# Attention scores and score maxima as products on quarters of TensorE's columns

## The chip, the cores and the metric

The kernel runs on one core of one Trainium2 chip. The metric is the device time of one execution in microseconds. Before the change it was 816.4, 816.55 and 818.32 us in three runs, median 816.55.

## The reference

The program is two decoder layers on 4 sequences of 256 tokens with 256 features, each layer an attention to a context of 1601 tokens, then a feed-forward part. The change lies in the attention of the second layer, which in the reference, with 16 heads of 16 features, is

```python
q = _qdq(x) @ _qdq(wq).T + bq
kv = cond @ wkv.T + bkv
k, v = jnp.split(kv, 2, axis=-1)
...
attn = jax.nn.softmax(jnp.einsum('bnhd,bmhd->bhnm', q, k) * scale, axis=-1)
o = jnp.einsum('bhnm,bmhd->bnhd', attn, v).reshape(B, N, C)
out = _qdq(o) @ _qdq(wp).T + bp
```

`_qdq` rounds to 8-bit integer steps, so the attention has to be exact to nearly float32. All of it has to be computed, over all 1601 keys; the second layer's feed-forward part follows.

## The kernel before

Queries and keys are each split into three bfloat16 parts, and six pairs of parts are stacked along the contraction (6 x 16 = 96 rows, `STACK_Q`, `STACK_K`), so that one bfloat16 product on 96 rows gives a float32-like score. `qst` holds the stacked queries of all sequences and heads, `kst` the stacked keys of two stages (a stage is half of the heads of one sequence).

The second layer's attention runs in a loop over 16 quads (four heads of one sequence) of 13 steps (`KT`, a tile of 128 keys, the last one of 65). In a step TensorE's stream holds, in this order:

- `scores` (L1066 to L1084): for each of four heads one product at L1080, stationary a tile of 128 keys (99 rows: three more carry minus the row maximum), moving the 256 queries of the head, output 128 x 256 into two PSUM banks that alternate by step. The first two heads, then the other two.
- `weigh` (L1086 to L1104) for the step before: the value products at L1101, float32. Each head has 17 stationary columns (16 values and a one for the denominator) and writes to its own group of 32 PSUM partitions, `bank(6)[32 * k:32 * k + VW]`; the four heads lie side by side on TensorE's columns. A float32 product is two instructions in the profile, so there are eight per step.
- `beside`: other work that a planner, `schedule` at L75, hands out by step: the keys (L878) and values (L888) of the next sequence, the transposes of the finished quad's output (`turn_out`, L1110), the tail of a finished sequence with its feed-forward part (`tail`, L1114 to L1187), and `shift` (L1056), which transposes the negated maxima on 3 columns at L1062. All but `shift` use 128 stationary columns.
- between these, `max_scores` (L978 to L991): the row maxima of the next quad need all scores once more, queries stationary, 128 x 400 or 401 keys to a product (L990), 32 of them to a quad. `pace` (L1222) places them evenly by the columns passed. They alternate between banks 0 and 1, and each waits until VectorE has reduced the last content of its bank.

The planner gives a step two to five maxima by the room it computes. The maxima for the first quad are made before the loop, in `first_maxima` (L993).

The other engines: VectorE reduces each block of maxima (L1669, `max_chunk`), forms the negated maxima after the last one of a quad (L1672 to L1680), and does the normalisation and the elementwise work of the tail. ScalarE makes the exponentials of a step in one instruction on 128 x 1024 (L1480, three buffers) and copies results from PSUM. GpSimd splits keys. SyncE issues all transfers. What a product waits for: scores of step i for the exponentials of step i - 2, value products for the exponentials of their step, a maximum for the reduction two before. Each group of products signals with its last instruction.

Of the kernel before, what the change touches and what calls it, by code (L numbers as in the profile page):

```python
# [27 lines left out]
P = 128  # L28
B, LQ, D = 4, 256, 256
# [20 lines left out]
HALF = H // 2  # L50
# [4 lines left out]
STACK_K = (0, 1, 0, 2, 0, 1)  # L55
SROWS = len(STACK_Q) * DH
VW = DH + 1
CH = [(0, 401), (401, 400), (801, 400), (1201, 400)]
MAGIC = float(1.5 * 2 ** 23)
LN_EPS = 1e-5  # L60
# [85 lines left out]
def program(nc, x_in, ctx_in, ctx0_in, seg_in, ident_in, tabs_in, kk_in, ones_in, wkvc_in, wkr_in, wkrs_in,  # L146
# [3 lines left out]
    with ExitStack() as ctx:  # L150
# [8 lines left out]
        def bank(i, n=1):  # L159
            return ps[:, i * 512:(i + n) * 512]  # L160
# [71 lines left out]
        kst = r1[:, 0:HALF * KEYS].bitcast(BF16).rearrange("p (r h k) -> p r h k", r=2, h=HALF)  # L232
        qst = r2[:, :].bitcast(BF16).rearrange("p (h t) -> p h t", h=H)
# [464 lines left out]
        def _(pe):  # L698
            mm = nc.tensor.matmul
# [7 lines left out]
            for c in range(FC):  # L707
                last = mm(bank(6), wkvc[:, c, :], ctx0[:, c, :], start=c == 0, stop=c == FC - 1)
            last.then_inc(kv_mm, 1)
            for b in range(B):  # L710
                for c in range(FC):
                    last = mm(bank(5)[:, b * KVC:(b + 1) * KVC], ctx0[:, c, b * K0:(b + 1) * K0], wkvc[:, c, 0:KVC],
                              start=c == 0, stop=c == FC - 1)
# [13 lines left out]
            for t in range(TILES):  # L727
# [3 lines left out]
                for c in range(FC):  # L731
                    last = nc.tensor.transpose(bank(2 + t % 2)[:, c * P:(c + 1) * P], xn[t % 2][:, c * P:(c + 1) * P],
                                               ident[:, :])
# [3 lines left out]
                if t >= 3 and t < 7:  # L737
                    for h in range(4 * (t - 3), 4 * (t - 3) + 4):
                        last = mm(bank(h // 8)[0:QC, (h % 8) * KVC:(h % 8 + 1) * KVC], wuq[:, h, :], wuk[:, h, :],
                                  start=True, stop=True)  # L740
# [6 lines left out]
            for hf in range(2):  # L747
                at = slice(hf * 512, (hf + 1) * 512)
                for h in range(H):
                    n = hf * H + h  # L750
# [7 lines left out]
                    if h % 2 == 1:  # L758
                        k = hf * (H // 2) + h // 2
                        if k >= 2:  # L760
                            pe.wait_ge(qb_ev, k - 1)
                        elif k == 1:
                            pe.wait_ge(kvt_ev, 1)
                        mm(bank(4 + k % 2), wqrs[:, h // 2, :], qcT[:, at], start=True,  # L764
                           stop=True).then_inc(qb_mm, 1)
# [209 lines left out]
                    last = nc.tensor.transpose(bank(7)[:, c * P:(c + 1) * P], qtok[:, c * P:(c + 1) * P], ident[:, :])  # L975
                last.then_inc(q1T_mm, 1)

            def max_scores(quad, n):  # L978

                b, s, u, c = quad // 4, quad // 2, n // len(CH), n % len(CH)  # L980
                h = 4 * (quad % 4) + u // 2
                ca = 8 * len(CH) * quad + n
                if n == 0:
                    pe.wait_ge(k_stk[quad % 4], 96 * (quad // 4 + 1))
                    pe.wait_ge(q_stk[b], 96)
                if ca >= 2:
                    pe.wait_ge(mx_rdy, ca - 1)
                a, m = CH[c]
                q0 = b * LQ + (u % 2) * P
                mm(bank(ca % 2)[:, 0:m], qst[0:SROWS, h, q0:q0 + P], kst[0:SROWS, s % 2, h % HALF, a:a + m],  # L990
                   start=True, stop=True).then_inc(mx_mm, 1)  # L991

            def first_maxima(t, third):  # L993

# [71 lines left out]
            def scores(quad, kt, first):  # L1066
                i, b, s = KT * quad + kt, quad // 4, quad // 2
                n = P if kt < KT - 1 else KLAST
                if first == 0:
                    if kt == 0:  # L1070
                        pe.wait_ge(sh_rdy, quad + 1)
                    if i == 0:
                        pe.wait_ge(ld_ones, 16)
                    if i == 1:
                        pe.wait_ge(v_ev, 2 * NV)
                    if i >= 2:
                        pe.wait_ge(ex_rdy, i - 1)
                for k in (first, first + 1):
                    h = 4 * (quad % 4) + k
                    last = mm(bank(2 + 2 * (i % 2), 2)[0:n, k * LQ:(k + 1) * LQ],  # L1080
                              kst[0:SROWS + 3, s % 2, h % HALF, kt * P:kt * P + n],
                              qst[0:SROWS + 3, h, b * LQ:(b + 1) * LQ], start=True, stop=True)
                if first == 2:
                    last.then_inc(sc_mm, 1)  # L1084

# [127 lines left out]
            for quad in range(QUADS + 2):  # L1213
                for kt in range(KT):
                    jobs = BESIDE.get((quad, kt), [])
                    maxima = [j for j in jobs if j[0] == "max"]
                    others = [j for j in jobs if j[0] != "max"]

                    total, count = step_work(others), len(maxima)
                    passed = [0]  # L1220

                    def pace(columns):  # L1222

                        passed[0] += columns
                        while maxima and (count - len(maxima)) * total < count * passed[0]:
                            max_scores(*maxima.pop(0)[1:])

                    if quad < QUADS:
                        pace(1)
                        scores(quad, kt, 0)  # L1230
                        pace(2 * LQ)
                        scores(quad, kt, 2)
                        pace(2 * LQ)
                        if quad or kt:
                            weigh(KT * quad + kt - 1)
                        pace(4 * LQ)
                    elif quad == QUADS and kt == 0:
                        weigh(STEPS - 1)
                    beside(others, pace)
                    while maxima:  # L1240
                        max_scores(*maxima.pop(0)[1:])


        @block.scalar
# [679 lines left out]
```

## Time and profile before

| | |
|---|---|
| median of 3 runs | 816.55 us (816.4 to 818.32) |
| the profiled execution | 814.17 us |
| its span | 812.4 us |
| TensorE busy | 753.3 us (93%), 5027 products |
| TensorE weight loads busy | 427.5 us (53%), 5027 |
| VectorE busy | 565.1 us (70%) |
| ScalarE busy | 383.6 us (47%) |
| GpSimd busy | 197.4 us (24%) |
| reductions of maxima (L1669) | 512 of 573 ns |
| exponentials (L1480) | 208 of 1024 ns |
| maxima (L990) | 512 of 341 ns |
| value products (L1101) | 1664 of 386 ns |
| scores (L1080) | 832 of 273 ns |

The profile is of one execution; times in it are counted from the start of its span. PE is TensorE, PEld its weight loads, DVE is VectorE, ACT ScalarE, POOL GpSimd, SP SyncE. The duration of a TensorE product runs from its start to the landing of its last column, and the next product starts before that; so the distance from start to start, not the duration, is what a product costs when the engine is full. "Busy" covers the durations, overlaps counted once. Idle time in brackets stands before the instruction, with what ended it.

### The profile page before, as it was taken

To read this page: it belongs to the slowest core of one execution; us is meant where nothing else is said; L and a number is where in the kernel's file an instruction comes from. 1 tells how busy PE (TensorE), PEld (TensorE's weight loads), DVE (VectorE), ACT (ScalarE), POOL (GpSimd) and SP (SyncE) were. 2 spreads that over 40 slices of the span, in tenths; PEclk is the share of its full clock that TensorE was granted. 3 is DMA by queue.
4 is the path that set the end of the run, shared out by engine and by line. 5 is a ranking of instruction groups with operands and counts; after the bars stand their busy time and mean duration, and the time that the engine had idled before them with its cause. 6 is when DMAs were issued, how large, how long until landed. Compare 5 with 4: busy or idle time off the path is not lost.

```text
span 812.4 us, 13087 instructions
## 1 busy us (share of the span) xinstructions
PE 753.3 (93%) x5027; PEld 427.5 (53%) x5027; DVE 565.1 (70%) x1290; ACT 383.6 (47%) x562; POOL 197.4 (24%) x208
## 2 busy tenths in 40 slices
PE   8999899978899989779999999999999999899996
PEld 4446677745556556554444455554455554345434
DVE  4887987712265675687787877777787777887814
ACT  2102435334333333216666666456665566574670
POOL 2497231312910321210310503100505002300000
PEclk9999999999999999989999999999999999999999
DMA  9300002004499142145065282650491810550000
GB/s 292 137 0 1 1 1 81 2 20 166 98 145 139 75 59 36 28 54 89 1 123 61 82 157 28 126 71 2 146 119 42 127 29 1 113 71 14 2 1 14
DMA packets 32476, 55.94 MB, mean 69 GB/s; under 512 B 11572, under 2 KB 20532, under 8 KB 31509
## 3 DMA queue, kind: packets, MB, share of 16 engines
q1 hardware_dynamic: 32408, 55.04, 34.2%
q8 instruction: 42, 0.69, 0.4%
q14 instruction: 26, 0.21, 0.1%
HBM read 42.56 MB, written 12.46 MB: 68 GB/s over the span
## 4 chain that ended last, share of the span: by engine, by line
PE 68%; DVE 18%; issue 6%; POOL 4%; ACT 2%; DMA 1%; SPq 0%; DVEq 0%; POOLq 0%; ACTq 0%
PE ps L1101 12%; PE ps L990 12%; PE ps L1080 9%; PE ps L878 6%; DVE small L1669 5%; PE ps L888 4%; PE ps L757 3%; PE ps L954 3%; PE ps L934 3%; PE ps L804 2%; PE ps L847 2%; PE ps L764 2%; PE ps L835 2%; DVE small L1619 1%; PE ps L1062 1%
## 5 line engine op out<-in xcount | busy, mean ns | idle before, releaser
L1669 DVE TENSOR_REDUCE small<-ps 128x1 f32<-128x400 f32 (+1 forms) x512 | 286.0, 573 | 82.6 <-PE ps L990 76.3
L1480 ACT ACTIVATE r<-ps 128x1024 f32<-128x1024 f32 (+1 forms) x208 | 212.6, 1024 | 89.1 <-PE ps L1080 86.1
L990 PE MATMUL ps<-r 96*128 96x400 bf16 (+1 forms) x512 | 170.8, 341 | 14.8 <-DVE small L1669 12.3
L1101 PE MATMUL ps<-r 128*17 128x256 f32 (+1 forms) x1664 | 130.7, 386 | 2.3 <-ACT r L1480 2.0
L1080 PE MATMUL ps<-r 99*128 99x256 bf16 (+1 forms) x832 | 126.0, 273 | 0.0
L990 PEld LDWEIGHTS ps<-r 96*128 96x128 bf16 x512 | 49.6, 97 | 126.9 <-DVE small L1669 93.3
L1080 PEld LDWEIGHTS ps<-r 99*128 99x128 bf16 (+1 forms) x832 | 81.5, 99 | 31.5 <-issue 9.3
L633 POOL TENSOR_TENSOR r<-r 128x400 bf16<-128x400 f32 (+1 forms) x32 | 29.4, 952 | 203.3 <-ACT r L1321 203.3
L934 PE MATMUL ps<-r,hT 128*128 128x512 f32 (+1 forms) x160 | 69.1, 564 | 0.0
L878 PE MATMUL ps<-r,wkvT 128*128 128x400 f32 (+1 forms) x128 | 53.3, 515 | 5.3 <-issue 5.3
L888 PE MATMUL ps<-wkvT,r 128*128 128x256 f32 (+1 forms) x208 | 57.1, 393 | 0.0
L1101 PEld LDWEIGHTS ps<-r 128*17 128x17 f32 (+1 forms) x1664 | 27.6, 95 | 51.8 <-issue 41.3
L622 POOL TENSOR_TENSOR r<-r,small 128x1024 f32<-128x1024 f32 x16 | 30.1, 1899 | 67.4 <-DVE small L1620 67.4
L614 POOL TENSOR_TENSOR r<-r 64x512 f32<-64x512 f32 x32 | 40.4, 1264 | 13.5 <-DVE r L1595 11.0
L1365 ACT ACTIVATE r<-ps,small 128x128 f32<-128x128 f32 x64 | 20.0, 364 | 50.1 <-DVE small L1646 27.6
L601 POOL TENSOR_TENSOR small<-small 128x1 f32<-128x1 f32 x24 | 14.0, 583 | 120.5 <-DVE small L1506 120.5
L888 PEld LDWEIGHTS ps<-wkvT,r 128*128 128x128 f32 (+1 forms) x208 | 39.1, 193 | 7.2 <-issue 0.3
L685 POOL TENSOR_TENSOR small<-small 128x2 f32<-128x2 f32 x4 | 2.8, 691 | 162.9 <-DVE small L1799 162.9
L1332 ACT ACTIVATE r<-ps 128x512 f32<-128x512 f32 (+1 forms) x28 | 15.9, 567 | 49.4 <-PE ps L888 49.3
L1303 ACT ACTIVATE r<-r 128x1024 f32<-128x1024 f32 x16 | 16.1, 1048 | 48.0 <-DVE r L1610 48.0
L1320 ACT ACTIVATE r<-ps,bk 128x400 f32<-128x400 f32 (+1 forms) x32 | 19.1, 597 | 41.3 <-PE ps L878 41.3
L934 PEld LDWEIGHTS ps<-r,hT 128*128 128x128 f32 x160 | 28.9, 196 | 18.3 <-issue 17.4
(201 smaller groups left out, 1023.9 us busy)
## 6 DMA issues: line engine op xcount, KB each, us to landing
r<-kscr SPq DMA_DIRECT2D x96, 200.1 KB, 8.8
kscr<-r SPq DMA_DIRECT2D x24, 400.2 KB, 4.0
r<-in_ctx_dram SPq DMA_DIRECT2D x4, 1601.0 KB, 6.9
r<-qscr SPq DMA_DIRECT2D x24, 128.0 KB, 5.2
r<-in_wo_dram SPq DMA_DIRECT2D x1, 2048.0 KB, 13.1
r<-in_gu_dram SPq DMA_DIRECT2D x1, 2048.0 KB, 7.7
qscr<-qpart SPq DMA_DIRECT2D x24, 64.0 KB, 1.7
x<-in_x_dram SPq DMA_DIRECT2D x1, 1024.0 KB, 5.4
```

The costliest lines, as they stand in the source:

```text
L614: nc.gpsimd.tensor_tensor(q, q, ropet[n % 2][at, :], ALU.add).then_inc(q_rdy, 1)
L622: nc.gpsimd.tensor_tensor(sm[t % 2][:, heads, :], sm[t % 2][:, heads, :], rec0[t % 2][:, heads].unsqueeze(2).to_broadcast([P, H // 2, K0]) ...
L633: last = nc.gpsimd.tensor_tensor(kpart[s][1][:, a:a + n], kf[s][:, a:a + n], kpart[s][0][:, a:a + n], ALU.subtract)
L757: mm(bank(n % 4), weff[:, h, :], qcT[:, at], start=True, stop=True).then_inc(qa_mm, 1)
L878: last = mm(bank(bnk)[:, 0:n], wkvT[:, k, (s % 2) * P:(s % 2 + 1) * P], ctxT[:, k, a:a + n], start=k == 0, stop=k == FC - 1)
L888: last = mm(bank(bnk)[0:n, (i % 2) * D:(i % 2 + 1) * D], ctxT[:, k, i * P:i * P + n], wkvT[:, k, D:2 * D], start=k == 0, stop=k == FC - 1)
L934: last = mm(bank(n % 3)[:, 0:w.shape[2]], hT[t % 2][:, k, :], w[:, k, :], start=k == 0, stop=k == FC - 1)
L990: mm(bank(ca % 2)[:, 0:m], qst[0:SROWS, h, q0:q0 + P], kst[0:SROWS, s % 2, h % HALF, a:a + m], start=True, stop=True).then_inc(mx_mm, 1)
L1080: last = mm(bank(2 + 2 * (i % 2), 2)[0:n, k * LQ:(k + 1) * LQ], kst[0:SROWS + 3, s % 2, h % HALF, kt * P:kt * P + n], qst[0:SROWS + 3, h, ...
L1101: last = mm(bank(6)[32 * k:32 * k + VW, 0:LQ], vx[0:n, b % 2, kt, h, :], pr[i % 3][0:n, k * LQ:(k + 1) * LQ], start=kt == 0, stop=kt == KT ...
L1480: fn(pr[i % 3][0:n, :], bank(2 + 2 * (i % 2), 2)[0:n, :], ACT.Exp, scale=SCALE1)\
L1669: v.tensor_reduce(mxc[quad % 2][:, n:n + 1], bank(ca % 2)[:, 0:m], AX_X, ALU.max).then_inc(mx_rdy, 1)
```

## The change

The scores and most of the maxima are issued as four products on 32 stationary columns each, that write to 32 PSUM partitions each, with the same moving operand; the value products have this form already. The last key tile (65 keys) is made of 32, 32 and 1. The maxima within the work of `beside` stay one product on 128 columns, as do those made before the loop; the others are parted. What is computed, the order of the work, the banks and the signals are the same: the last of the four products signals.

```diff
+QUARTER = P // 4
...
-            def max_scores(quad, n):
+            def max_scores(quad, n, parted=False):
...
-                mm(bank(ca % 2)[:, 0:m], qst[0:SROWS, h, q0:q0 + P], kst[0:SROWS, s % 2, h % HALF, a:a + m],
-                   start=True, stop=True).then_inc(mx_mm, 1)
+                width = QUARTER if parted else P
+                for r in range(0, P, width):
+                    last = mm(bank(ca % 2)[r:r + width, 0:m], qst[0:SROWS, h, q0 + r:q0 + r + width],
+                              kst[0:SROWS, s % 2, h % HALF, a:a + m], start=True, stop=True)
+                last.then_inc(mx_mm, 1)
...
                 for k in (first, first + 1):
                     h = 4 * (quad % 4) + k
-                    last = mm(bank(2 + 2 * (i % 2), 2)[0:n, k * LQ:(k + 1) * LQ],
-                              kst[0:SROWS + 3, s % 2, h % HALF, kt * P:kt * P + n],
-                              qst[0:SROWS + 3, h, b * LQ:(b + 1) * LQ], start=True, stop=True)
+                    for r in range(0, n, QUARTER):
+                        z = min(r + QUARTER, n)
+                        last = mm(bank(2 + 2 * (i % 2), 2)[r:z, k * LQ:(k + 1) * LQ],
+                                  kst[0:SROWS + 3, s % 2, h % HALF, kt * P + r:kt * P + z],
+                                  qst[0:SROWS + 3, h, b * LQ:(b + 1) * LQ], start=True, stop=True)
...
-                    def pace(columns):
+                    def pace(columns, parted=False):
 
                         passed[0] += columns
                         while maxima and (count - len(maxima)) * total < count * passed[0]:
-                            max_scores(*maxima.pop(0)[1:])
+                            max_scores(*maxima.pop(0)[1:], parted)
 
                     if quad < QUADS:
-                        pace(1)
+                        pace(1, parted=True)
                         scores(quad, kt, 0)
-                        pace(2 * LQ)
+                        pace(2 * LQ, parted=True)
                         scores(quad, kt, 2)
-                        pace(2 * LQ)
+                        pace(2 * LQ, parted=True)
                         if quad or kt:
                             weigh(KT * quad + kt - 1)
-                        pace(4 * LQ)
+                        pace(4 * LQ, parted=True)
                     elif quad == QUADS and kt == 0:
                         weigh(STEPS - 1)
                     beside(others, pace)
                     while maxima:
-                        max_scores(*maxima.pop(0)[1:])
+                        max_scores(*maxima.pop(0)[1:], True)
```

## Rows read from the trace of the kernel before

**Rows 1.** The page, busy time and instructions of each engine.

```profile
PE 753.3 (93%) x5027; PEld 427.5 (53%) x5027; DVE 565.1 (70%) x1290; ACT 383.6 (47%) x562; POOL 197.4 (24%) x208
```

**Rows 2.** Busy time by stretch, the whole loop: start:end, length, then busy by engine.

```profile
core 0: us, PE busy (x) PEld busy (x) DVE busy (x) ACT busy (x) POOL busy (x), PEclk, DMA share, GB/s
369.76:789.20 419.44, 406.55 (x3438) 203.17 (x3438) 319.41 (x701) 265.69 (x308) 68.00 (x75) 1.00 0.38 67
```

**Rows 3.** The chain of waits in order of time: start, length, what.

```profile
515.00 0.56 PE ps L1101 x8
515.55 0.28 PE ps L990
515.83 0.44 PE ps L1080 x4
516.27 0.17 PE ps L990
```

**Rows 4.** Timeline of TensorE, 513.8 to 515.5: start, length, engine, line, idle before.

```profile
513.84 0.38 PE L888 MATMUL ps<-wkvT,r 128*128 128x256 f32 x1
514.05 0.34 PE L990 MATMUL ps<-r 96*128 96x400 bf16 x1
514.23 0.60 PE L1080 MATMUL ps<-r 99*128 99x256 bf16 x4
514.66 0.34 PE L990 MATMUL ps<-r 96*128 96x400 bf16 x1
...
514.93 0.41 PE L1101 MATMUL ps<-r 128*17 128x256 f32 x4
...
514.93 0.63 PE L1101 MATMUL ps<-r 128*17 128x256 f32 x8
...
514.93 0.13 PEld L1101 LDWEIGHTS ps<-r 128*17 128x17 f32 x8 [0.27 <-issue]
515.48 0.10 PEld L990 LDWEIGHTS ps<-r 96*128 96x128 bf16 x1 [0.42 <-DVE small L1669]
```

**Rows 5.** Timeline of TensorE around a shift of the maxima, 695.0 to 696.0.

```profile
695.11 0.34 PE L990 MATMUL ps<-r 96*128 96x400 bf16 x1 [1.62 <-DVE small L1669]
695.39 0.61 PE L1062 MATMUL ps<-identb,nst 128*3 128x128 bf16 x8
695.93 0.34 PE L990 MATMUL ps<-r 96*128 96x400 bf16 x1
```

**Rows 6.** The page, costliest groups: count, busy, mean ns, idle before.

```profile
L1669 DVE TENSOR_REDUCE small<-ps 128x1 f32<-128x400 f32 (+1 forms) x512 | 286.0, 573 | 82.6 <-PE ps L990 76.3
...
L1101 PE MATMUL ps<-r 128*17 128x256 f32 (+1 forms) x1664 | 130.7, 386 | 2.3 <-ACT r L1480 2.0
```

**Rows 7.** Timeline of VectorE, 370.6 to 371.9.

```profile
370.70 1.19 DVE L1669 TENSOR_REDUCE small<-ps 128x1 f32<-128x400 f32 x2 [0.98 <-PE ps L990]
```

**Rows 8.** Busy time by stretch, each from value products to later ones, columns as rows 2.

```profile
369.76:371.20 1.44, 1.44 (x14) 0.64 (x14) 0.50 (x1) 0.92 (x2) 0.00 (x0) 1.00 1.25 112
766.10:767.55 1.45, 1.45 (x16) 0.64 (x15) 1.19 (x3) 0.81 (x2) 0.00 (x0) 1.00 0.00 0
371.20:373.05 1.85, 1.80 (x17) 0.73 (x16) 1.56 (x4) 1.25 (x2) 0.00 (x0) 1.00 1.27 108
384.62:385.89 1.27, 1.27 (x14) 0.54 (x13) 1.01 (x3) 0.73 (x1) 0.00 (x0) 1.00 0.04 13
738.74:740.01 1.27, 1.27 (x14) 0.54 (x13) 0.98 (x3) 0.96 (x1) 0.00 (x0) 1.00 0.00 0
781.24:783.52 2.28, 2.27 (x24) 0.88 (x24) 0.00 (x0) 2.05 (x2) 0.00 (x0) 1.00 0.00 0
```

**Rows 9.** Timeline of ScalarE in the last quad, 782.4 to 783.0.

```profile
782.45 1.02 ACT L1480 ACTIVATE r<-ps 128x1024 f32<-128x1024 f32 x1 [0.16 <-PE ps L1080]
```

**Rows 10.** Line L1062: duration in ns, minimum, median, maximum.

```profile
L1062 PE MATMUL ps<-identb,nst x128: 216/219/311, 364.8 to 771.7; 128*3 128x128 bf16 x128
```

**Rows 11.** The page, DMA queue that carries instructions: packets, MB, share.

```profile
q8 instruction: 42, 0.69, 0.4%
```

## Prediction

> **What bounds the kernel now.** I read the page first. TensorE is busy for 93% of the span, VectorE for 70%, ScalarE for 47% [rows 1]. The loop that the change is in runs from 369.76 to 789.20 us: 208 steps in 419.4 us, 2.02 us a step, on 16 quads of 13 steps, at a granted clock of 1.00 [rows 2]. "Busy" includes modelled ends, so next I took the chain of an undisturbed stretch apart, piece by piece, to see how long TensorE takes per piece and what it should take.
>
> A step with no other work and two maxima is, from 515.00 on, value products 0.56, maximum 0.28, four scores 0.44, maximum 0.17: 1.45 us, again and again, and TensorE stands in every piece [rows 3]. The two maxima are the same product and cost 0.17 or 0.28: the dear one follows the value products. The timeline shows why. A maximum (L990) at 514.05 is followed by scores 0.18 later, but the one at 514.66 by value products 0.27 later: 0.09 more. Of the eight value instructions (two passes for float32, four heads in four groups of 32 columns) four take 0.41 and eight 0.63, so the second pass starts about 0.21 after the first and is through with its columns another 0.21 later, at 0.42; the next weights are only loaded at 0.55 (515.48), and that load is no longer hidden: about 0.12 more. "Idle before" confirms it: 0.27 to 0.42 us without a weight load at either change [rows 4]. It is not float32 that costs: L888 at 513.84, float32 on all columns, is followed by a bfloat16 maximum 0.21 later, the time of its stream. Eight transposes on 3 columns start at 695.39 and a full-width product follows at 695.93; eight at the 0.055 worked out below are 0.44, so again 0.10 is lost [rows 5, 10]. So TensorE pays about 0.1 us each time it goes from products on all columns to products on a quarter, or back, and twice a step.
>
> **Part by part.** (1) Removed: changes of form. Following the order of emission in the code, I count 442 changes in the loop before and 149 after; those left stand around keys, values, turned outputs and the tail's products, which stay on all columns. 293 x 0.1 = 29 us of TensorE's time. That is not the gain, because other engines are close behind.
>
> (2) What comes next. VectorE's reduction takes 573 ns [rows 6]; two in a row take 1.19 us, so the pitch is 0.61, and an interval with three maxima lasts 1.85 us = 3 x 0.61 from one group of value products to the next: VectorE already sets it [rows 7, 8]. So by interval between value products:
> - Without full-width work, two maxima: 58 intervals of 1.44 or 1.45, the first from 369.76, the last from 766.10 [rows 8]. TensorE would need 0.42 + 0.44 + 2 x 0.17 = 1.20, VectorE needs 2 x 0.61 = 1.23. VectorE takes over: 0.21 saved each, 12.2 us.
> - The same with one maximum: 24 intervals of 1.27 to 1.38, the first from 384.62, the last from 738.74 [rows 8]. TensorE 1.03; ScalarE's exponentials, 1.02 each, come in pairs, and each pair waits for scores, which wait behind a maximum and the value products; I take 1.12. 0.15 saved, 3.6 us.
> - The last quad has no maxima: 2.28 for two steps, with ScalarE 0.16 idle between pairs [rows 8, 9]. The gap loses the 0.11 of one change; pitch 1.08 for 1.14, on 12 intervals: 0.7 us.
> - Three maxima (9 intervals), the steps with VectorE's long work (bias, scale) and the 15 with the shift of the maxima: nothing. At the shift, VectorE works off small operations after the last maximum, and TensorE's next maximum waits for it, 1.62 us in the case shown [rows 5]; the change reaches none of them.
> - The 74 intervals with full-width work: two changes before, two after. Nothing.
> Sum: 16.5 us.
>
> (3) Added: 2432 score products (832 become 3264; the last key tile has three parts, 32, 32 and 1) and 1263 for the 421 maxima that are parted; 59 maxima between full-width products and the 32 before the loop stay whole. Each brings a weight load, so 7390 instructions. What do they cost? Streams: the four groups of the value products start together (four in 0.41, where one alone has 386 ns in the mean [rows 4, 6]), so four quarters stream in the time of one if they don't share a limit; 0.11 for 256 columns, 0.17 for 400. Issue: eight weight loads of L1101 in 0.13 us, where the one of L990 has 0.10 alone [rows 4]: some 5 ns apart, and the products no more. From this end the cost is nil. The other end is the transposes on 3 columns: 0.61 for eight with 219 ns each is (0.61 - 0.22) / 7 = 0.055 a pair [rows 5, 10]; but 128 columns at 0.11 per 256 stream for 0.055 too, so that row is explained by its stream. I take the nearer row, the value products: quarters in the same four groups. Against it I set the stagger: the fourth group ends 0.02 after the first, which the 74 intervals that still change form pay, 1.5 us. That leaves 15. Waits: none is added, and only the fourth part signals, as one product did; nothing is moved past SP's or POOL's queues. Instructions fetched: 42 packets of 0.69 MB now for 10,054 loads and products [rows 1, 11], so some 30 packets more, at most one for each 5 us in quiet stretches; nothing in the trace is seen to wait for the present ones, and if that ends, each packet may cost a microsecond or so.
>
> **Forecast:** 15 us less. The profiled execution took 814.17 us for its span of 812.4, so 799.1; from the median of 816.55, 801.5. A measurement of this kernel can tell about 0.3% (2.4 us) from no change. Its own range: all 29 us is an end that VectorE's pitch excludes; 21 if waits at other places shrink too (795.5), 9 if quiet intervals meet other waits (807.5).
>
> **Rivals.** A, issue: a quarter's pair costs TensorE more than 27 ns, and four no longer fit in a score's 0.108. The place is the scores of every step, full-width ones too. With 0.055 a pair, the far end: scores 16 x 0.055 = 0.88 for 0.43, +94 us over 208 steps; maxima 0.22 for 0.17, +21; changes -29; less some 13 hidden where VectorE sets the interval: +73, so 890. It decides from about 32 ns a pair: (32 - 27) x 16 x 208 = 17 us, the whole gain. For it: no stretch shows more than eight narrow pairs together; a quiet step would need 32 pairs in 1.23 us, 38 ns each, and the queue may have been full in the bursts seen. Against it: those bursts are over five times faster. The Trainium skill, "TensorE: Matmul & The Clock Gate", under "Wait — 56ns, not 53.3ns?", says that with hardware decode off a matmul costs some 62 ns of microcode. By that rule, as an estimate, the scores alone would be 0.99 us a step, +116 us in all. The transposes at 0.055 a pair are below it, so the trace speaks against that mode. Chance 0.13.
>
> A2, streams: four bfloat16 quarters together get only the columns per time that four float32 ones get, 256 in 0.21. Scores +0.42 a step (+87), maxima +0.17 each (+70), changes -29: some 940. The bytes per time are those already seen, which speaks against it. 0.04.
>
> B, the cover is thinner: VectorE, at 1.19 of 1.44 us in quiet intervals, with its chains at shift and bias gives back half of the 12.2: 16.5 - 6.1 - 1.5 = 9 us or less saved, 807.5 to 813. 0.14.
>
> C, nothing: the drain belongs to the value products themselves (17 columns, float32), whatever stands beside them, so none goes. The transposes (3 columns, bfloat16) that lose the same 0.10 speak against it. 816 to 818. 0.07.
>
> **Chances.** Forecast 0.62, B 0.14, C 0.07, A 0.13, A2 0.04: faster by over 0.3% 0.76, within 0.07, slower 0.17. The range leaves out A and A2 and reaches to C: 795 to 817.
>
> **What would show it.** Value products followed by a maximum 0.42 to 0.45 after their start, with no 0.42 without a weight load; the three-line pattern of quiet intervals at 1.23 instead of 1.44, with VectorE's reductions 0.61 apart and the waits of L990 for VectorE longer in sum; last quad at 1.08; intervals with keys or values as long as before. A is right if the four parts of a score start more than 0.11 apart from the next head's and the product groups grow without an engine to wait for; C if 0.56 and 0.28 stand as they are. The forecast is wrong if the reductions stay further apart than 0.61 in quiet intervals though TensorE no longer changes form.

## The result and the profile after

The changed kernel is slower: 830.44 us (829.09 to 832.08, 4 runs) beside 816.47 (815.43 to 818.32, 4 runs) for the kernel before, a ratio of 1.0169 with a 95% interval of 1.0146 to 1.0191. The forecast was 801.5 in a range of 795 to 817. The profiled execution took 829.25 us, of which the span is 827.4 at a mean granted clock of 0.977; the kernel before had 814.17, 812.4 and 0.985. A few executions are longer at a lower granted clock whatever the kernel (824.91 us in one of 19 of the kernel before), and the ratios leave them out; of the version with quarters for the scores alone (below) that leaves one execution of four, 839.84 us.

In the lines that follow, the reductions of maxima are L1675 (L1669 before), the maxima L993 (L990), the scores L1086 (L1080), the value products L1107 (L1101), the exponentials L1486 (L1480), keys and values L879 and L889 (L878 and L888); in the kernels of the experiments some stand 2 to 10 lines further down. First the page of the kernel after: busy time, the instruction queue and the chain that ended last.

```profile
PE 740.6 (89%) x8721; PEld 458.0 (55%) x8722; DVE 569.0 (69%) x1290; ACT 381.8 (46%) x562; POOL 197.5 (24%) x208
...
q8 instruction: 71, 1.16, 0.6%
...
PE 56%; issue 18%; DVE 17%; POOL 4%; ACT 3%; DMA 1%; SPq 0%; POOLq 0%; DVEq 0%; ACTq 0%
```

Beside [rows 1] and [rows 11]: TensorE has 8721 products for 5027, and is busy for 12.7 us less although the span is 15 us longer. So it isn't TensorE's work that grew. VectorE's reductions (L1675) take the same 573 ns each. What did grow is the fetched code, 71 packets for 42, and "issue" on the chain, time in which an engine waits for nothing that the profile shows. The same line of the page of the kernel before had a third of it:

```profile
PE 68%; DVE 18%; issue 6%; POOL 4%; ACT 2%; DMA 1%; SPq 0%; DVEq 0%; POOLq 0%; ACTq 0%
```

**Where nothing interferes, the change does what was forecast.** The chain of waits of the kernel after through a quiet stretch (start, length, what), to be read against [rows 3]:

```profile
405.93 0.43 PE ps L1107 x8
406.37 0.17 PE ps L993 x4
406.54 0.44 PE ps L1086 x16
406.98 0.17 PE ps L993 x4
407.15 0.43 PE ps L1107 x8
```

Value products are followed by a maximum 0.43 us after their start, not 0.56, and no maximum costs 0.28 any more. One step is 407.15 - 405.93 = 1.22 us for 1.45. Busy time by stretch, with the columns of [rows 2], has the same step, an interval with three maxima, and the whole loop:

```profile
411.06:412.28 1.22, 1.22 (x36) 0.81 (x36) 1.15 (x3) 1.02 (x1) 0.00 (x0) 1.00 0.38 147
...
371.02:372.67 1.65, 1.58 (x43) 0.79 (x36) 1.58 (x4) 1.02 (x1) 0.00 (x0) 1.00 1.27 111
...
369.79:804.90 435.11, 395.19 (x7097) 234.24 (x7101) 323.29 (x701) 264.03 (x308) 68.11 (x75) 0.98 0.36 66
```

The loop takes 435 us for 419 [rows 2], and its granted clock is 0.98, not 1.00. The gain of the quiet steps is eaten somewhere else, and the clock points to stretches in which TensorE had fallen idle.

**Where the time went.** The same chain 20 us later:

```profile
426.21 0.21 PE ps L1086 x5
426.42 5.57 issue
431.99 0.83 PE ps L1086 x9
432.82 0.34 PE ps L993 x3
433.15 0.85 PE ps L1107 x6
```

In the middle of a head's scores TensorE stops for 5.57 us, no engine is waited for, and after it every piece takes twice its time: 0.85 for 0.43, 0.34 for 0.17. The stretches say why (the third column from the end is the granted clock):

```profile
426.42:431.99 5.57, 0.00 (x1) 0.00 (x1) 0.47 (x1) 0.00 (x0) 0.00 (x0) 0.83 1.06 123
432.00:436.90 4.90, 4.90 (x68) 3.65 (x72) 1.86 (x4) 2.05 (x2) 0.00 (x0) 0.50 0.96 115
```

During the gap the clock falls (0.83 in the mean), and for the 4.9 us after it it is 0.50, TensorE's level of 1.2 GHz instead of 2.4. There are five gaps of more than 1 us in the loop in which TensorE waits for no engine ("issue"), and none in the kernel before. In the timeline of TensorE they stand in brackets, as idle time before the first instruction behind them:

```profile
378.88 0.40 PE L1107 MATMUL ps<-r 128*17 128x256 f32 x3 [1.53 <-issue]
...
431.99 0.83 PE L1086 MATMUL ps<-r 99*32 99x256 bf16 x11 [5.57 <-issue]
...
496.73 0.52 PE L993 MATMUL ps<-r 96*32 96x400 bf16 x3 [4.02 <-issue]
...
619.28 0.34 PE L993 MATMUL ps<-r 96*32 96x401 bf16 x1 [1.49 <-issue]
...
739.10 0.52 PE L993 MATMUL ps<-r 96*32 96x401 bf16 x3 [5.98 <-issue]
```

Their sum is 18.6 us, and the three long ones are each followed by a stretch at a granted clock of 0.50, of 4.9, 5.0 and 5.0 us. What those stretches hold takes half of that at 1.00, so they cost another 7.5 us. Without both, the loop would take 435.1 - 18.6 - 7.5 = 409.0 us (an estimate), 10 less than before.

**What TensorE lacks is instructions.** The transfers of the kernel after from 415.3 to 428.2 (queue, kind: packets, MB, share of 16 engines):

```profile
q1 hardware_dynamic: 556, 1.45, 89.2%
...
r<-kscr SPq DMA_DIRECT2D x12, 200.1 KB, 10.6
```

There is no row for q8, the queue that carries instructions: no packet starts in 12.9 us. The first one starts in the next 0.2 us, at 428.24:

```profile
q8 instruction: 1, 0.02, 57.9%
```

It takes some 1.85 us (57.9% of 16 engines for 0.2 us), so it has landed at about 430.1, and TensorE goes on at 431.99. The other gaps end in the same way, 2.4 to 3.8 us after a packet starts.

A packet is 1.16 MB / 71 = 16 KB. The kernel has (20476 - 13087) = 7389 instructions more in 29 packets more, so 255 to a packet. A quiet step now issues 32 products and 32 loads in 1.22 us, so TensorE uses up a packet in 4.9 us. What moves meanwhile are the twelve reads of the stacked keys, 2.4 MB, which SyncE issues in one burst; its timeline:

```profile
416.35 5.48 SPq L549 DMA_DIRECT2D r<-kscr  x12
```

The kernel before has the same burst, and the trace had it too. Its transfers from 411.2 to 434.4:

```profile
q1 hardware_dynamic: 1265, 3.39, 91.2%
```

No packet starts for 23 us there either. But its quiet step issues 14 products and 14 loads in 1.45 us, so a packet lasts it 13 us.

A stretch without a packet isn't yet a late packet, since none may be due. How late one comes shows in the counts of products and loads before it, set against the same kernel without the key reads (below). There the packet of this place starts at 422.2 us, after 4994 products and loads. The kernel after had come as far at 420.8, but its packet starts at 428.24: 7.5 us late. It issued 226 more, until 426.4, and stopped. In the kernel before, the packet of the stretch starts without the reads after 3948 products and loads; with them it had come as far at 425.06, and the packet starts at 434.44, 9.4 us late. But 226 more instructions last it until about 438.7, so the packet is there in time. The delay is the same or longer; what differs is how long TensorE can go on.

### The profile page after: what moved, and what is told of

Its sections match the earlier page's. It is cut to its first block, busy times and chain, and to the rows that moved or that the text cites. A ratio compares the mean times of both kernels' runs of the same rounds, so it can differ in the third digit from the quotient of the medians.

```text
span 827.4 us, 20476 instructions
## 1 busy us (share of the span) xinstructions
PE 740.6 (89%) x8721; PEld 458.0 (55%) x8722; DVE 569.0 (69%) x1290; ACT 381.8 (46%) x562; POOL 197.5 (24%) x208
## 3 DMA queue, kind: packets, MB, share of 16 engines
q8 instruction: 71, 1.16, 0.6%
## 4 chain that ended last, share of the span: by engine, by line
PE 56%; issue 18%; DVE 17%; POOL 4%; ACT 3%; DMA 1%; SPq 0%; POOLq 0%; DVEq 0%; ACTq 0%
PE ps L993 9%; PE ps L1107 7%; PE ps L1086 6%; PE ps L879 6%; PE ps L889 4%; DVE small L1675 4%; PE ps L758 3%; PE ps L955 3%; PE ps L935 3%; PE ps L805 2%; PE ps L848 2%; PE ps L765 2%; ACT r L1486 2%; PE ps L836 1%; DVE small L1625 1%
## 5 line engine op out<-in xcount | busy, mean ns | idle before, releaser
L1675 DVE TENSOR_REDUCE small<-ps 128x1 f32<-128x400 f32 (+1 forms) x512 | 286.7, 573 | 94.1 <-PE ps L993 86.4
L1486 ACT ACTIVATE r<-ps 128x1024 f32<-128x1024 f32 (+1 forms) x208 | 210.9, 1023 | 103.8 <-PE ps L1086 101.1
L993 PE MATMUL ps<-r 96*32 96x400 bf16 (+3 forms) x1775 | 186.6, 343 | 28.5 <-DVE small L1675 14.7
L1107 PE MATMUL ps<-r 128*17 128x256 f32 (+1 forms) x1664 | 135.0, 388 | 7.0 <-ACT r L1486 4.6
L1086 PE MATMUL ps<-r 99*32 99x256 bf16 (+1 forms) x3264 | 132.5, 276 | 7.1 <-issue 6.0
L993 PEld LDWEIGHTS ps<-r 96*32 96x32 bf16 (+1 forms) x1775 | 57.5, 95 | 107.3 <-DVE small L1675 52.7
L1086 PEld LDWEIGHTS ps<-r 99*32 99x32 bf16 (+1 forms) x3264 | 91.2, 97 | 30.5 <-issue 6.9
L634 POOL TENSOR_TENSOR r<-r 128x400 bf16<-128x400 f32 (+1 forms) x32 | 29.4, 952 | 208.4 <-ACT r L1327 208.4
L879 PE MATMUL ps<-r,wkvT 128*128 128x400 f32 (+1 forms) x128 | 55.8, 535 | 5.4 <-issue 5.1
L1107 PEld LDWEIGHTS ps<-r 128*17 128x17 f32 (+1 forms) x1664 | 44.7, 98 | 27.4 <-ACT r L1486 16.0
L889 PE MATMUL ps<-wkvT,r 128*128 128x256 f32 (+1 forms) x208 | 58.4, 399 | 0.0
L889 PEld LDWEIGHTS ps<-wkvT,r 128*128 128x128 f32 (+1 forms) x208 | 38.0, 192 | 12.5 <-issue 4.8
L935 PEld LDWEIGHTS ps<-r,hT 128*128 128x128 f32 x160 | 28.9, 196 | 18.3 <-issue 17.3
L1326 ACT ACTIVATE r<-ps,bk 128x400 f32<-128x400 f32 (+1 forms) x32 | 19.1, 596 | 42.2 <-PE ps L879 42.2
```

The lines of the kernel that those rows point to most:

```text
L634: last = nc.gpsimd.tensor_tensor(kpart[s][1][:, a:a + n], kf[s][:, a:a + n], kpart[s][0][:, a:a + n], ALU.subtract)
L879: last = mm(bank(bnk)[:, 0:n], wkvT[:, k, (s % 2) * P:(s % 2 + 1) * P], ctxT[:, k, a:a + n], start=k == 0, stop=k == FC - 1)
L889: last = mm(bank(bnk)[0:n, (i % 2) * D:(i % 2 + 1) * D], ctxT[:, k, i * P:i * P + n], wkvT[:, k, D:2 * D], start=k == 0, stop=k == FC - 1)
L935: last = mm(bank(n % 3)[:, 0:w.shape[2]], hT[t % 2][:, k, :], w[:, k, :], start=k == 0, stop=k == FC - 1)
L993: last = mm(bank(ca % 2)[r:r + width, 0:m], qst[0:SROWS, h, q0 + r:q0 + r + width], kst[0:SROWS, s % 2, h % HALF, a:a + m], start=True, st ...
L1086: last = mm(bank(2 + 2 * (i % 2), 2)[r:z, k * LQ:(k + 1) * LQ], kst[0:SROWS + 3, s % 2, h % HALF, kt * P + r:kt * P + z], qst[0:SROWS + 3, ...
```

## Experiments

The expectations call theory F (fetch) S, for supply, and rival G I; in those for the three kernels with less added code, F stands for the price of a change of form instead.

**Theory F (fetch):** an instruction packet asked for during the burst of key reads comes late; TensorE, which now uses a packet in some 5 us of quiet steps, runs dry, and the pause takes the clock along. Rival G: the narrow pairs themselves cost more than their streams. Rival T: the burst slows the transfers or the memory as such, and the kernel before would gain from its absence as well. All medians stand beside those of the kernel before, run on the same chip.

**The reads one at a time, in both kernels.** SyncE waits for the landing of each read before it issues the next.

```diff
                                 .then_inc(k_stk[quad % 4], 16)
+                        if s >= 2:
+                            sp.wait_ge(k_stk[quad % 4], 96 * (quad // 4) + 16 * (g + 1))
```

After:

> The changed kernel, but each of the 12 reads of restacked keys (200 KB each) waits for the landing of the one before, so that the DMA queues never hold more than one. Theory S (instruction supply: TensorE runs dry because its instruction packets queue behind these bursts; the quarter form itself does what was forecast): the gaps of 2 to 6 us on TensorE that end shortly after a late instruction packet go, and with them the stretches at half clock behind them; 797 to 806 us. Rival I (the quarters themselves cost TensorE more, or the gaps have another cause): 827 to 833 us. Rival K (keys come too late when paced): slower than 833, with TensorE waiting for restacked keys.

Before:

> The same pacing in the kernel before, as control. Theory S: with 256 instructions to a packet and fewer than half as many used per us, nothing ran dry before, so 815 to 818 us. Rival: if the bursts slow the kernel before too (through SBUF or queues), some us less, and then e1's gain is partly this.

Measured: the kernel after 819.87 (815.78 to 821.15), the one before 825.05 (822.92 to 827.63), beside 816.38; ratios 1.0043 (1.0013 to 1.0074) and 1.0114 (1.0077 to 1.015). So one edit makes the one kernel 10.6 us faster and the other 8.7 us slower, and no gap above 1 us without an engine or a transfer to wait for is left in either. Both miss their expectations (797 to 806, and 815 to 818), because the keys now come late. The waits of TensorE (in total, times, longest), of the kernel after:

```profile
PE ps L995 <- DMA r<-kscr: 10.9, 3, 7.0
```

The kernel before has 9.6 us of the same wait. Some 10 us of new waits in each: the test was blunt, though its direction speaks for F and against T.

**No reads at all, in both kernels.** The stages from the third on take the keys that the first two left in place; the twelve reads of each of those stages aren't made, so the scores of the later sequences are of other keys.

```diff
-                        sp.wait_ge(k_stk[quad % 4], 96 * (s // 2))
+                        sp.wait_ge(k_stk[quad % 4], 96)
...
-                    for g, j in enumerate(STACK_K):
+                    for g, j in enumerate(STACK_K if s < 2 else ()):
...
-                    pe.wait_ge(k_stk[quad % 4], 96 * (quad // 4 + 1))
+                    pe.wait_ge(k_stk[quad % 4], 96)
```

After:

> The changed kernel without the reads that restack keys for stages 2 to 7 (the scores of later sequences are then made from the first stages' keys: that part of the computation is left out). Theory S: as paced or 1 to 3 us better, 796 to 803 us, no gap without an engine to wait for. Rival I: 825 to 832 us.

Before:

> The same reads left out of the kernel before, as control. Theory S: within 3 us of the kernel before, 813 to 817 us. If it gains much more, the bursts cost something besides instruction supply.

Measured: after 808.12 (807.11 to 808.56), ratio 0.9909 (0.9884 to 0.9934); before 816.71 (814.09 to 821.22), ratio 1.0016 (0.9995 to 1.0038), beside 816.38. The reads cost the kernel before nothing that can be measured and the kernel after 22 us. The kernel after is 5 us above the 796 to 803 that was expected without them, since other losses stay (below). This rules out T, and as the only explanation it rules out G, since the pairs are all still there. In this run the loop takes 411 us. One gap is left, 1.56 us at 380.

**Less added code.** Three kernels change the form of a part only. Quarters for the scores, whole maxima (4864 instructions more than before, 638 changes of form for 149):

```diff
-                width = QUARTER if parted else P
+                width = P
```

> Scores as quarters, all maxima whole. By the order of emission that is 638 changes of form in the loop, against 442 before and 149 with both parted; 4864 more instructions than before. Theory F (what a quarter saves is the change of form, about 0.1 us each, where nothing else sets the step): the scores alone lose, up to 20 us for the 196 changes more, and some instruction gaps beside: 828 to 845 us, quiet steps with two maxima at 1.55 to 1.7 us. Rival P (quarters are faster by themselves, whatever stands beside them): below 816.

Whole scores, quarters for the maxima (2526 more, 563 changes):

```diff
-                    for r in range(0, n, QUARTER):
-                        z = min(r + QUARTER, n)
+                    for r in range(0, n, P):
+                        z = min(r + P, n)
```

> Maxima as quarters, scores whole: 563 changes of form, 2526 more instructions than before. Theory F: quiet steps with two maxima keep two changes (maximum to scores, scores to maximum) and stay near 1.44, those with three get more; 815 to 828 us. Rival P: about half of the gain of both parts, 808 to 812.

Halves of 64 columns for both:

```diff
-QUARTER = P // 4
+QUARTER = P // 2
```

> Scores and maxima on halves (64 columns) instead of quarters. Theory F in its strict form (any change of the width of the groups costs, also 64 to 32): 442 changes around the value products stay and 149 between halves and full width come, 820 to 835 us. Rival: only full width against less costs, then quiet steps are 1.22 as with quarters, with a third of the added instructions, and it is fast: 800 to 808 us.

Measured, beside 815.65: maxima only 838.87 (834.4 to 847.41), ratio 1.0321 (1.0248 to 1.0393); halves 868.47 (863.89 to 870.81), ratio 1.0634 (1.0587 to 1.0682); scores only 853.81 (839.84 to 854.61), without a ratio; 839.84 lies in the range expected (828 to 845), the median doesn't. The other two came out beyond what was expected, 815 to 828 and 820 to 835. Their chains in the same stretch, at a granted clock of 1.00 in all three, tell what they have in common. Scores only:

```profile
405.31 0.28 PE ps L993
405.58 0.55 PE ps L1086 x16
406.13 0.28 PE ps L993
406.41 0.56 PE ps L1107 x8
```

Maxima only:

```profile
405.30 0.54 PE ps L1086 x4
405.85 0.28 PE ps L993 x4
406.13 0.43 PE ps L1107 x8
406.56 0.17 PE ps L993 x4
```

Halves:

```profile
406.23 0.44 PE ps L1086 x8
406.67 0.17 PE ps L993 x2
406.84 0.56 PE ps L1107 x8
407.39 0.29 PE ps L993 x2
```

Whatever comes in front of a change of form costs 0.11 to 0.12 more: four changes give steps of 1.67 us, two give 1.43, none 1.22. That is the price of the prediction, shown on scores (0.55 for 0.44), maxima (0.28 for 0.17) and value products (0.56 for 0.43). The halves show more: going from 64 columns to 32 is a change too, so the halves save nothing in a quiet step (0.44 + 0.17 + 0.56 + 0.29 = 1.46). As to the gaps, the maxima alone have none, the scores alone two, 3.18 us before 495.70 and 3.68 before 630.67. None, two and five gaps at 2526, 4864 and 7389 instructions more go the way of F, though the two of the scores are counted in an execution of 853.24 us. The halves don't fit that row: with 2505 more they have two gaps of 3.93 and 2.07 us, where the maxima alone have none. Where the ends of packets fall beside the bursts may count as well, not the number alone; that was not tried by itself.

The size of the two misses is explained only in part. By intervals between value products, the loop of the maxima alone grows by 19.1 us, and its 74 intervals with full-width work by 20.3. The 121 changes of form more that the count gives are worth 14 us at 0.115 each (an estimate), which leaves 6 to the loads behind changes that the last experiment is about. The loop of the halves grows by 53.0 us: 24.4 in the same 74 intervals, 18.3 in the 15 with the shift of the maxima, one of which holds the gap of 2.07. The latter is more than its 149 further changes account for, and no run here says why.

**The reads in groups of three, in both kernels.** SyncE waits after each third read, so that no more than three are queued, and the keys still come nearly in time (TensorE waits 0.3 us for them in all).

```diff
                                 .then_inc(k_stk[quad % 4], 16)
+                        if s >= 2 and g % 3 == 2:
+                            sp.wait_ge(k_stk[quad % 4], 96 * (quad // 4) + 16 * (g + 1))
```

After:

> The changed kernel with the restacking reads issued by threes: after each third read the queue waits until the three have landed. Three reads of 200 KB are short enough in the queues for the instruction packets to pass in time, and six are there earlier than one by one, so TensorE should not wait for keys as it did one by one (7 us before the last batch). Theory S: 803 to 810 us, near the 808 us without reads. Rival: the gaps are at the start of a burst whatever its length, then 815 to 825.

Before:

> The kernel before with its restacking reads by threes: control for the run of the changed kernel by threes (806.7 us). Theory S: the kernel before never ran out of instructions, so 814 to 819 us. If it comes near 807 too, the pacing is the gain and not the quarters.

Measured: after 806.68 (805.34 to 809.67), ratio 0.9903 (0.9871 to 0.9936) beside 815.65; before 816.45 (814.16 to 824.83), ratio 1.0026 (0.9996 to 1.0057) beside 815.59. All twelve reads are made and no product is changed, and 23.8 us are gone. The transfers of the stretch that had no instruction packet, 415.3 to 428.2:

```profile
q1 hardware_dynamic: 537, 1.42, 63.2%
q8 instruction: 2, 0.03, 1.3%
```

As many bytes, and two packets among them. And the loop, busy time by stretch:

```profile
371.45:780.66 409.21, 387.89 (x7093) 229.56 (x7093) 322.53 (x701) 264.03 (x308) 68.05 (x75) 1.00 0.35 70
```

The mean clock is 1.00 again, and the loop takes 409.2 us, 10.2 less than in the kernel before. Of the gaps above 1 us without an engine to wait for one is left, 1.11 at 380. This is F as closely as it can be had without touching the products.

**A longer burst, in both kernels.** Every second group of six reads is followed by six more into a spare tensor, eighteen in a row.

```diff
+                    if s >= 2 and quad % 2 == 1:
+                        sp.wait_ge(dumped, 96 * (s - 2))
+                        for g, j in enumerate(STACK_K):
+                            sp.dma_start(kdum[g], kscr[s % 2, j].rearrange("(h d) k -> d h k", d=DH)[:, heads])\
+                                .then_inc(dumped, 16)
...
```

After:

> The changed kernel with longer bursts: behind the second six restacking reads of each stage from 2 on, the same six reads once more into a spare DRAM tensor that nobody uses, 18 reads in a row for 12. Theory S: the queues are full half as long again, so instruction packets come later and TensorE stands longer: 850 to 880 us. Rival (the gaps have to do with SBUF writes of the keys, or with the keys' arrival): 829 to 836.

Before:

> The same longer bursts in the kernel before. Theory S: a packet of 256 instructions lasts it 15 to 20 us in quiet stretches, a burst of 18 reads takes some 20 us, so it begins to run dry itself, but less: 817 to 835 us, at least 15 us less added than in the changed kernel.

Measured, beside 815.59: after 831.87 (826.97 to 836.4), ratio 1.0212 (1.015 to 1.0273); before 816.35 (813.39 to 819.75), ratio 1.0011 (0.9991 to 1.0031). A miss in both (850 to 880 and 817 to 835 were expected): half as many reads again hardly add to the gaps. And 831.87 lies in the range of the rival, by which the gaps come from the arrival of the keys or their writes to SBUF (829 to 836).

```profile
432.33 0.83 PE L1096 MATMUL ps<-r 99*32 99x256 bf16 x11 [5.86 <-issue]
...
497.53 0.52 PE L1003 MATMUL ps<-r 96*32 96x400 bf16 x3 [5.12 <-issue]
```

5.57 became 5.86, and 4.02 became 5.12; the one of 5.98 that ended at 739.10 gave way to one of 3.41 that ends at 731.80. The time thus doesn't decide between F and that rival. The counts of products and loads up to the gaps do, of the kernel after and then of this one:

```profile
0.00:430.00 430.00, 383.21 (x2610) 244.13 (x2610) 282.52 (x653) 153.97 (x293) 139.72 (x144) 0.98 0.34 74
0.00:495.00 495.00, 440.85 (x3627) 278.27 (x3627) 329.52 (x750) 193.45 (x340) 150.74 (x156) 0.98 0.36 77
```

```profile
0.00:430.00 430.00, 381.73 (x2610) 242.37 (x2610) 280.50 (x653) 153.97 (x293) 139.67 (x144) 0.98 0.35 75
0.00:495.00 495.00, 438.81 (x3627) 276.18 (x3627) 327.45 (x750) 193.46 (x340) 150.65 (x156) 0.98 0.37 79
```

TensorE stops behind exactly the same instruction in both, 5220 and 7254 products and loads into the program. Between those two places lie 2034, which is 8 x 254, and the later gaps lie on the same grid: in the kernel after at 11,064 (15 x 254 further) and 14,877 (15 x 254.2 further), in this one at 11,064 and at 14,624, one packet sooner. So TensorE stops where a packet of code ends, as F has it; keys that arrive at some time don't come in such steps.

A packet doesn't wait until the whole burst is through. The six reads more are issued from 421.57 on, when TensorE had passed the usual place for this packet (420.8), and the packet starts at 428.69, for 428.24. That it waits for what stands in the queues when it is asked for would explain this, but the trace doesn't show when it is asked for, so that stays argued. The kernel before, whose packets last 13 us, stands the longer burst too.

**Whole maxima beside full-width work.** The trace of the kernel with the reads in threes has one loss left that the forecast had at 1.5 us only: intervals with full-width work got longer. In it, a parted maximum is followed by the keys' product (TensorE, then its weight load):

```profile
448.28 0.34 PE L995 MATMUL ps<-r 96*32 96x400 bf16 x4
...
448.55 0.94 PE L881 MATMUL ps<-r,wkvT 128*128 128x400 f32 x2
```

```profile
448.55 0.30 PEld L881 LDWEIGHTS ps<-r,wkvT 128*128 128x128 f32 x2 [0.38 <-ACT r L1329]
```

and in the kernel before, where the maximum is whole and follows the value products:

```profile
449.32 0.34 PE L990 MATMUL ps<-r 96*128 96x400 bf16 x1
...
449.50 0.84 PE L878 MATMUL ps<-r,wkvT 128*128 128x400 f32 x2
...
449.39 0.30 PEld L878 LDWEIGHTS ps<-r,wkvT 128*128 128x128 f32 x2
```

The number of changes is the same, but they come in front of another product. Behind a change the weight load is not hidden, and that of the float32 keys is the dear one: keys follow a maximum 0.27 later, not 0.18. The last version therefore leaves a maximum whole where full-width work follows in the same place (72 maxima, 216 pairs less, 149 changes as before), with the reads in threes.

```diff
+            def wide(jobs):
+                return any(kind(j) in ("k", "v", "out", "turn_o", "project", "turn_x", "up", "gate", "down", "expert")
+                           for j in jobs)
+
...
-                        pace(4 * LQ, parted=True)
+                        pace(4 * LQ, parted=not wide(others))
```

> The changed kernel by threes, with the maxima between value products and full-width work whole again: 72 maxima, 216 product and load pairs less, and the same 149 changes of form. In the run by threes the 74 intervals with full-width work grew by 0.08 us each, since a float32 weight load of 0.19 us now stands unhidden behind a change of form where a bfloat16 one of 0.10 stood before. Theory W: most of these 6 us come back: 800 to 803 us. Rival: another load or wait takes its place, 805 to 808.

Measured: 801.06 (798.88 to 805.97), ratio 0.9826 (0.9779 to 0.9874) beside 815.59. The pair is back as it was:

```profile
448.53 0.34 PE L995 MATMUL ps<-r 96*128 96x400 bf16 x1
...
448.71 0.84 PE L881 MATMUL ps<-r,wkvT 128*128 128x400 f32 x2
```

This version beats both kernels, the one before by 14.5 us and the changed one by 29.4. It is 5.6 us below the one with the reads in threes, with ranges that just touch (805.34 to 805.97), so that step rests on the pair above and on the intervals in the table below as well.

## Why the prediction was wrong

**The step that failed** is the sentence on instructions fetched: "nothing in the trace is seen to wait for the present ones, and if that ends, each packet may cost a microsecond or so". It named the right place, the right count (30 packets more, 29 came) and the right rate (one for each 5 us in quiet stretches), and was then costed at nil, without the test that it called for: what the transfers do in 5 us. The trace of before had the hint, since it shows 23 us without a packet behind the burst of key reads. A packet that comes 7.5 us late, where the instructions in hand last 5.6, is a gap of several microseconds. The cover was not that packets are prompt (that one came 9.4 us late in the kernel before) but that the instructions in hand lasted longer. And the price wasn't a microsecond for each of 29 packets, but 18.6 us in five gaps, with 7.5 us in the three stretches at the lower clock on top. Between the loops of the changed kernel and of the one with the reads in threes lie 25.9 us (435.1 and 409.2): the gaps make 17.5 of them (18.6 less 1.1), the lower clock 7.5, which leaves 0.9.

The Trainium skill, "Runtime: NRT & Kernel Launch", under "Instruction fetch mechanics", says that the sequencer fetches its code in blocks of 16 KiB, 256 instructions, over a DMA queue of its own, and that the cost of this is "mostly hidden". The size agrees with the rows here (255 to a packet); "hidden" held for the kernel before and not for this one.

**The changes of form** at 0.1 us each: right. The quiet interval with two maxima went from 1.44 to 1.22 (forecast 1.23), value products are followed by a maximum 0.43 later (forecast 0.42 to 0.45), and the three partial versions show the same price at two and four changes a step. But 1.22 is not what the forecast made it of. It had VectorE take over with 2 x 0.61; TensorE stands in every piece of the chain (0.43 + 0.17 + 0.44 + 0.17), and VectorE is busy for 1.15 of the 1.22. That the two sums come so close, 1.22 and 1.23, is luck.

**What comes next.** With the reads in threes, I sorted the intervals of the loop between value products by what they hold, and set them against the kernel before (one profiled execution each, so single numbers are good to a microsecond at best):

| intervals | forecast, us | reads in threes | and whole maxima |
|---|---|---|---|
| quiet, two maxima | -12.2 | -5.7 | -5.2 |
| quiet, one maximum | -3.6 | -1.5 | -1.6 |
| last quad | -0.7 | -0.7 | -0.7 |
| three maxima | 0 | -1.8 | -1.8 |
| VectorE's other long work | 0 | -2.5 | -2.0 |
| shift of the maxima | 0 | -4.3 | -4.7 |
| full-width work | +1.5 | +6.4 | +1.5 |
| rest | 0 | 0 | +0.9 |
| sum | -15 | -10.2 | -13.6 |

- The quiet intervals gave far less than their term, as rival B had it. The row holds 51 of them, of which 28 lose the full 0.22; the others lie beside waits for VectorE. All 58 that the forecast counted give 6.9 of 12.2 us, the seven not in the row standing in rows below.
- VectorE's pitch of 0.61 was misread. It came from two reductions in a row; a long row of them in the kernel with the reads in threes has 7.50 / 13 = 0.577:

```profile
405.56 7.50 DVE L1677 TENSOR_REDUCE small<-ps 128x1 f32<-128x400 f32 x13
```

  So 1.85 for three maxima [rows 8] was not VectorE's limit. It held two changes of form as well, and the nine such intervals lost 0.20 each, to 1.65.
- The intervals at the shift gained 4.3 where nothing was forecast. Perhaps VectorE's small operations start earlier when the maxima ahead of them do; no run tests it.
- The 74 intervals with full-width work cost 6.4 where 1.5 was set; "two changes before, two after" counted the changes and not what stands behind them.

**The rivals.** A (issue over 27 ns a pair) fell: sixteen pairs follow each other in 0.44 us, 27.5 ns each, step after step. The 62 ns of microcode for a matmul that the Trainium skill ("TensorE: Matmul & The Clock Gate", "Wait — 56ns, not 53.3ns?") gives for hardware decode switched off are not what this trace shows. A2 (shared streams) fell by the same row, C (the drain stays) by the 0.43. The chance of 0.17 on the slower side lay wholly on A and A2: right sign, wrong mechanism. The one that decided was in the text, but as an afterthought and not as a rival with a price.

That the last version ends at 801.06, beside a forecast of 801.5, is partly chance: the terms of the table missed in both directions, and its reads are issued in another way.

## What to carry to other kernels

An edit that multiplies instructions multiplies the rate at which code is fetched: divide the time of a stretch by its instructions / 255 to get what a packet lasts, and compare it with how late a packet comes behind the largest burst of transfers. Here that was 7.5 to 9.4 us, and another 2.4 to 3.8 from its start until TensorE went on. A long stretch without a packet is only a hint: the kernel before had 23 us of it at 13 us a packet and never stopped. Where a packet lasts less than the delay, break up the bursts first; here a wait after each third 200 KB read was worth 23.8 us and cost the kernel before nothing that could be measured. Count changes of form by what stands behind them too, since each left a weight load unhidden here (0.27 us to the keys' product for 0.18).

## What the hardware showed that was not expected

- Instruction packets come late behind 2.4 MB of the kernel's own reads, by 7.5 us in the kernel after and 9.4 in the one before. TensorE stops where a packet's instructions end, at multiples of 254 products and loads, and "issue" on the chain for microseconds, in the middle of a group of products, is the sign.
- The pauses of 5.57, 4.02 and 5.98 us took TensorE to 1.2 GHz (granted clock 0.50 from 432.00 to 436.90), and steps cost twice as much until it came back; after the pauses of 1.5 us in that run the granted clock stayed at 1.00. In the run with the longer burst a pause of 1.78 us was followed by 0.50 from 620.42 to 623.82.
- Products on 64 columns and products on 32 are different forms: the change costs the same 0.11 us.
- The gaps don't grow with the burst (5.57 to 5.86 us for half as many reads again). What a packet waits for remains open. The gap of 1.1 to 1.6 us at 380 us, which stays in every version with quarters for both whose reads are absent or in threes, stands on the same grid (3439 products and loads, 7 x 254.4 before 5220) and ends 2.4 us after a packet starts. Another burst lies before it: six reads of queries (128 KB each) and three of weights (256 KB each), issued from 369.0 to 373.7 us. It is thus likely of the same kind, but no run here changes that burst.
